# Quantised gate and up weights of a two-layer transformer kernel: integers made by TensorE transposes, or from a second load in the transposed layout

## The reference

```python
h_q = (rmsnorm(x) @ w_q.T); h_k = (ctx @ w_k.T); h_v = (ctx @ w_v.T)      # per head
x = x + hidden + softmax(h_q h_k^T + position_bias, masked) @ h_v @ w_out.T

def fake_quant(t, axis):
    s = jnp.max(jnp.abs(t), axis=axis, keepdims=True) / QMAX
    s = jnp.maximum(s, 1e-08)
    return jnp.clip(jnp.round(t / s), -QMAX - 1.0, QMAX) * s

gate = fake_quant(y, -1) @ fake_quant(w_gate, 1).T
up = fake_quant(y, -1) @ fake_quant(w_up, 1).T
x = x + fake_quant(silu(gate) * up, -1) @ fake_quant(w_down, 1).T
```

## Time and profile before

| what | us |
|---|---|
| median of 3 runs | 1104.09 |
| lowest and highest of them | 1101.44 and 1105.84 |
| the profiled execution | 1102.04 |
| its span, first to last instruction | 1100.3 |

### The profile page before, as it was taken

The page is one execution under the profiler, slowest core; times in us unless marked ns, Lnnn a source line. Parts: engine busy times, 40 slices in busy tenths (PEclk is TensorE's granted clock), DMA queues, the critical chain, the costliest instruction groups (busy, mean ns, idle before and its releaser), DMA issues. The chain is left out here.

```text
span 1100.3 us, 18306 instructions
## 1 busy us (share of the span) xinstructions
PE 999.7 (91%) x6010; PEld 844.0 (77%) x6010; DVE 706.1 (64%) x1844; ACT 515.7 (47%) x1330; POOL 469.3 (43%) x362
## 2 busy tenths in 40 slices
PE   4999999999999999999999999999999999565465
PEld 3888888888888888888888888888878887333353
DVE  6566565656576767586555665665676575587384
ACT  3454444444444554445543543553555344167251
POOL 5554444444444545434444354353444352344200
PEclk9999999999999999999999999999999999799577
DMA  6433333323333323334232132222212220000002
GB/s 205 146 94 94 95 95 93 94 93 95 93 96 96 92 89 97 117 99 133 59 105 82 32 104 70 72 82 82 72 62 82 82 63 23 20 1 1 1 1 77
DMA packets 50412, 87.71 MB, mean 80 GB/s; under 512 B 6368, under 2 KB 15200, under 8 KB 50336
## 3 DMA queue, kind: packets, MB, share of 16 engines
q1 hardware_dynamic: 50336, 86.76, 25.5%
HBM read 84.64 MB, written 2.10 MB: 79 GB/s over the span
## 5 line engine op out<-in xcount | busy, mean ns | idle before, releaser
L540 POOL TENSOR_TENSOR wq_lo<-raw_q,wq_hi 128x512 fp32r<-128x512 f32 x64 | 82.8, 1293 | 263.6 <-DVE prob L1213 257.3
L1493 PE MATMUL pX<-wv_lo,cT_hi 128*128 128x256 f32 x512 | 149.3, 292 | 0.2 <-ACT q_sb L678 0.2
L1196 DVE TENSOR_TENSOR score<-pS,b_mask 128x512 f32<-128x512 f32 x64 | 44.2, 691 | 161.4 <-PE pS L1671 148.1
L802 ACT ACTIVATE prob<-score,neg_max 128x128 f32<-128x128 f32 x256 | 99.7, 391 | 97.2 <-DVE neg_max L1199 97.2
L1494 PE MATMUL pX<-wv_hi,cT_lo 128*128 128x256 f32 x512 | 144.0, 281 | 0.0
L1495 PE MATMUL pX<-wv_hi,cT_hi 128*128 128x256 f32 x512 | 144.0, 281 | 0.0
L540 POOL TENSOR_TENSOR wv_lo<-raw_v,wv_hi 128x1024 fp32r<-128x1024 f32 x32 | 77.6, 2425 | 124.9 <-ACT wv_hi L678 124.9
L678 ACT ACTIVATE v_sb<-pX 128x512 f32<-128x512 f32 x64 | 38.2, 597 | 163.2 <-PE pX L1495 163.2
L1493 PE MATMUL pX<-xT_lo,wq_hi 128*128 128x512 f32 x256 | 106.0, 414 | 6.1 <-POOL wq_lo L540 5.1
L1493 PE MATMUL oacc<-wo_lo,aT_hi 128*128 128x512 f32 x256 | 100.5, 393 | 5.1 <-DVE aT_lo L1191 3.8
L1493 PE MATMUL pX<-cT_lo,wk_hi 128*128 128x512 f32 x256 | 105.0, 410 | 0.0
(11 more groups left out here) (276 smaller groups left out, 2387.1 us busy)
## 6 DMA issues: line engine op xcount, KB each, us to landing
raw_k<-in_wk SPq DMA_DIRECT2D x64, 256.0 KB, 2.9
raw_q<-in_wq SPq DMA_DIRECT2D x64, 256.0 KB, 3.5
raw_v<-in_wv SPq DMA_DIRECT2D x32, 512.0 KB, 4.2
raw_o<-in_wo SPq DMA_DIRECT2D x64, 256.0 KB, 2.7
b_raw<-in_bias SPq DMA_DIRECT2D x64, 64.0 KB, 2.8
g_raw<-in_w_gate SPq DMA_DIRECT2D x16, 172.0 KB
g_raw<-in_w_up SPq DMA_DIRECT2D x16, 172.0 KB
f_raw<-in_w_down SPq DMA_DIRECT2D x4, 688.0 KB, 4.7
```

The costliest lines, as they stand in the source:

```text
L540: g.tensor_tensor(w_lo[c][:], w_raw[c][:], w_hi[c][:].bitcast(F32), ALU.subtract).then_inc(s_w_lo[c], 1)
L802: e = a.activation(prob[:, b, :], score[:, b, :], ACT.Exp, bias=neg_max[:, b:b + 1], accum_out=row_sum[:, b:b + 1])
L1196: v.tensor_tensor(score[:], pS[:].rearrange("p (b s) -> p b s", b=HB), b_mask[:], ALU.add).then_inc(s_scored, 1)
L1493: mm(dst, lh, rl, start=start, stop=False, skip_group_check=lint)
```

## The change

The host passes the gate and up weights a second time, transposed: partition p holds, for each of four blocks of 128 input columns, the 86 weights of a slice (`rows_across`). Each of steps 0 to 31 loads such a slice too (`load_across`, 128 x 344 f32, 172 KB), behind the load of `raw_k`, once `s_g_mag` says that the slice before has been used. The load of `g_raw` now waits for the maximum alone (`s_g_max`). `g_mag`, `g_q` and their instructions go, as do the reciprocal at L1178 and TensorE's four transposes with their wait. VectorE instead runs `scaled_rows` at the end of its step: when ScalarE has copied the spread steps (`s_g_out`), it takes the reciprocal of 86 of them on all partitions, multiplies the transposed weights by it, and adds the rounding constant. ScalarE takes the constant off one step later and writes `w_rowT` straight from SBUF. VectorE's loop over groups of four steps covers steps 4 to 15 instead of 4 to 19; the rest is written out.

```diff
--- before.py
+++ after.py
@@ -70,8 +70,9 @@
         g_raw = sbuf("g_raw", [P, D])
-        g_mag = sbuf("g_mag", [P, D])
-        g_q = sbuf("g_q", [P, D], BF16)
+        gT_raw = sbuf("gT_raw", [P, KT, FR])
+        g_scaled = sbuf("g_scaled", [P, KT, FR])
+        g_inv = sbuf("g_inv", [P, 1, FR])
...
@@ -438,8 +440,14 @@
             def load_rows(i, src, t):
 
                 if later(i):
+                    sp.wait_ge(s_g_max, i)
+                sp.dma_start(g_raw[0:FR, :], src[t]).then_inc(s_g_in, 16)
+
+            def load_across(i, srcT, t):
+
+                if later(i):
                     sp.wait_ge(s_g_mag, i)
-                sp.dma_start(g_raw[0:FR, :], src[t]).then_inc(s_g_in, 16)
+                sp.dma_start(gT_raw[:], srcT[t]).then_inc(s_gT_in, 16)
...
             load_rows(0, w_gate, 0)
+            load_across(0, w_gateT, 0)
             context(1)
...
                 if unless_last(n + 2):
                     load("k", n + 2, head2)
+                if rows is not None and later(n):
+                    load_across(n, (w_gateT, w_upT)[rows], n - rows * (H // 2))
                 if odd and unless_last(n + 3):
...
@@ -816,12 +827,11 @@
-                if rows is not None:
-
-                    act.wait_ge(s_g_mag, n + 1)
-                    if later(n):
-                        act.wait_ge(s_g_trans, n)
-                    a.activation(g_q[0:FR, :], g_mag[0:FR, :], ACT.Copy, bias=-MAGIC).then_inc(s_g_q, 1)
+                if later(n) and (rows is not None or n == H):
+                    whose = (n - 1) // (H // 2) if isinstance(n, int) else rows
+                    act.wait_ge(s_g_mag, n)
+                    a.activation(w_rowT[whose][:, :, rows_of(n - 1 - whose * (H // 2))], g_scaled[:], ACT.Copy,
+                                 bias=-MAGIC).then_inc(s_g_int, 1)
...
                 if rows is not None:
                     cols = rows_of(n - rows * (H // 2))
-                    act.wait_ge(s_g_trans, n + 1)
-                    copy(w_row[rows][:, cols], pX1[:, 0:FR])
-                    copy(w_rowT[rows][:, :, cols],
-                         g_trans_bank[:, 0:KT * FR].rearrange("p (k r) -> p k r", k=KT)).then_inc(s_g_out, 1)
+                    act.wait_ge(s_g_row, n + 1)
+                    copy(w_row[rows][:, cols], pX1[:, 0:FR]).then_inc(s_g_out, 1)
...
@@ -1171,26 +1179,33 @@
                 dve.wait_ge(s_g_in, 16 * (n + 1))
-                v.tensor_reduce(f_s[0:FR, 0:1], g_raw[0:FR, :], AX.X, ALU.max, apply_absolute_value=True)
+                v.tensor_reduce(f_s[0:FR, 0:1], g_raw[0:FR, :], AX.X, ALU.max,
+                                apply_absolute_value=True).then_inc(s_g_max, 1)
                 dve.drain()
                 v.tensor_scalar(f_s[0:FR, 1:2], f_s[0:FR, 0:1], 1.0 / QMAX, 1e-8, ALU.mult, ALU.max)
                 dve.drain()
-                v.reciprocal(f_s[0:FR, 2:3], f_s[0:FR, 1:2])
                 if later(n):
-                    dve.wait_ge(s_g_trans, n)
+                    dve.wait_ge(s_g_row, n)
                 v.tensor_scalar(f_diag[0:FR, 0:FR], ident[0:FR, 0:FR], f_s[0:FR, 1:2], None,
                                 ALU.mult).then_inc(s_g_diag, 1)
-                dve.drain()
+
+            def scaled_rows(n, whose):
+
+                dve.wait_ge(s_g_out, n + 1)
+                v.reciprocal(g_inv[:, 0, :], w_row[whose][:, rows_of(n - whose * (H // 2))])
+                dve.drain()
+                dve.wait_ge(s_gT_in, 16 * (n + 1))
                 if later(n):
-                    dve.wait_ge(s_g_q, n)
-                v.tensor_scalar(g_mag[0:FR, :], g_raw[0:FR, :], f_s[0:FR, 2:3], MAGIC,
-                                ALU.mult, ALU.add).then_inc(s_g_mag, 1)
+                    dve.wait_ge(s_g_int, n)
+                v.tensor_tensor(g_scaled[:], gT_raw[:], g_inv[:].to_broadcast([P, KT, FR]), ALU.mult)
+                dve.drain()
+                v.tensor_scalar(g_scaled[:], g_scaled[:], MAGIC, None, ALU.add).then_inc(s_g_mag, 1)
...
@@ -1241,21 +1256,23 @@
                         v.tensor_scalar(top_flat[:, tile], pick[:, r, ::-1], LOWEST, None, ALU.not_equal)
+                if rows is not None:
+                    scaled_rows(n, rows)
                 early_end(n)
                 second_x_end(n)
                 if isinstance(n, int) and n in (1, H - 1):
                     add_norm(n // (H - 1))
...
-            quad(0)
-            with dve.Fori(1, SECOND_X // 4 - 1) as q:
-                quad(q)
-            for q in range(SECOND_X // 4 - 1, H // 4):
-                quad(q)
+            quad(0, 0)
+            with dve.Fori(1, H // 8) as q:
+                quad(q, 0)
+            for q in range(H // 8, H // 4):
+                quad(q, 1)
...
@@ -1718,12 +1735,8 @@
                     pe.wait_ge(s_k, n + 2)
-                    mm(pX1[:, 0:FR], ones[0:FR, :], f_diag[0:FR, 0:FR], start=True, stop=True)
-                    pe.wait_ge(s_g_q, n + 1)
-                    for kt in range(KT):
-                        last = tr(g_trans_bank[:, kt * FR:(kt + 1) * FR], g_q[0:FR, kt * P:(kt + 1) * P],
-                                  ident_b[0:FR, 0:FR])
-                    last.then_inc(s_g_trans, 1)
+                    mm(pX1[:, 0:FR], ones[0:FR, :], f_diag[0:FR, 0:FR], start=True,
+                       stop=True).then_inc(s_g_row, 1)
...
+    def rows_across(w):
+
+        return w.reshape(H // 2, FR, KT, P).transpose(0, 3, 2, 1)
```

More of the change, by code:

```diff
@@ L50, in layers_kernel @@
 def layers_kernel(nc, x, cT, mask, bias, ln_w, wq, wk, wv, wo, w_gate, w_up, w_down,
-                  conv_w, gamma, beta, router_w, router_b, lora_a, lora_b, out):
+                  w_gateT, w_upT, conv_w, gamma, beta, router_w, router_b, lora_a, lora_b, out):
     ctx = ExitStack()
@@ L284, in layers_kernel @@
         s_g_in = sem("g_in")
+        s_gT_in = sem("gT_in")
         s_g_mag = sem("g_mag")
+        s_g_max = sem("g_max")
+        s_g_row = sem("g_row")
         s_g_out = sem("g_out")
         s_g_proj = sem("g_proj")
-        s_g_q = sem("g_q")
-        s_g_trans = sem("g_trans")
+        s_g_int = sem("g_int")
         s_gate = sem("gate")
@@ L396, in layers_kernel @@
         h_blocks = range(6), range(6, IT)
-        g_trans_bank = pX1[:].bitcast(BF16)[:, NH:2 * NH]
         def later(n):
@@ L1191, in attended_low, with step @@
                 v.tensor_tensor(aT_lo[:], pT[:], aT_hi[:].bitcast(F32), ALU.subtract).then_inc(s_a_lo, 1)
-            def step(n, half, q, j, rows=False):
+            def step(n, half, q, j, rows=None):
                 dve.wait_ge(s_b_mask, n + 1)
@@ L1201, in step @@
                     attended_low(n - 1)
-                if rows:
+                if rows is not None:
                     rows_of_gate(n)
@@ L1247, in step, with quad @@
                     add_norm(n // (H - 1))
-            def quad(q):
+            def quad(q, rows):
                 for j in range(4):
-                    step(4 * q + j, 0, q, j, rows=True)
+                    step(4 * q + j, 0, q, j, rows)
             dve.wait_ge(s_cT_lo, KT)
-            quad(0)
-            with dve.Fori(1, SECOND_X // 4 - 1) as q:
-                quad(q)
-            for q in range(SECOND_X // 4 - 1, H // 4):
-                quad(q)
+            quad(0, 0)
[3 more added lines that the diff above has]
+                quad(q, 1)
             dve.wait_ge(s_cT_lo, 2 * KT)
@@ L1922 @@
         "w_down": host("L0_ffn_w_down"),
+        "w_gateT": rows_across(host("L0_ffn_w_gate")),
+        "w_upT": rows_across(host("L0_ffn_w_up")),
         "conv_w": rows(host("L1_xattn_conv_w")),
```

## The result

| | before | after |
|---|---|---|
| median of the runs made together (4 each), us | 1102.97 | 1117.2 |
| lowest and highest of them | 1101.44 and 1105.84 | 1116.52 and 1118.47 |
| the profiled execution, and its span | 1102.04, 1100.3 | 1117.56, 1115.7 |

After against before is 1.0134, with a 95% interval of 1.0111 to 1.0157: slower by about 14 us. That is the sign that was forecast, and 4 us more than 1113.

A forecast was written before the change was run, and what follows sets the result against it. TensorE's list of matmuls was taken to set the time (busy 91%). Terms -6.7 + 4.5 + 11.9 = +9.7 us gave 1111.7 on the profiled execution, 1113.8 on the median, stated as 1113; range 1102 to 1122.

The forecast's parts named there:

- The transposes, -6.7 us: TensorE, seams of steps 0 to 31: removing four transposes gains 0.21 us a step, 6.7 us in all.
- The reciprocal, 0.74 us between 0.25 and 0.91: VectorE's new reciprocal of 86 elements: taken at 0.74 us, 0.25 at the least, 0.91 at the most.
- rival 1: Reciprocal slower, 0.8 to 0.9 us: steps 0.31 us late, total +15.1 us, 1119 to 1123; chance 0.22.
- rival 2: Hardly any change: reciprocal 0.25 us, `add_norm` keeps its turn, 6.6 us lost against 6.7 gained, 1104; chance 0.22.
- Rival 3: Faster: cover before TensorE needs `aT_lo` is wider, hiding nearly all new work, 1097.5 us; chance 0.08.
- Ordinary steps, 0.14 us late: VectorE at each step's end: 1.80 us of new work against 1.66 available, 4.5 us over 32 steps.
- Steps 20 to 22, 2.4 + 0.6 us: VectorE's statistics of steps 20 and 21 (2.4 us) and aggregation of step 22 (0.6) now stand behind `scaled_rows` and are lost.
- Step 1 and step 31, 3.8 and 3.1 us: `add_norm` behind `scaled_rows`: 1.9 us if VectorE keeps its turn, 5.6 and 4.3 if GpSimd gets in; midpoints taken.
- Step 0, 2.0 us: New multiply and add fall beside GpSimd's `wk_lo` and `cT_lo`: between 0 and 2.6 us lost, 2.0 taken.
- The loads, nothing: SyncE's 32 added loads of 172 KB arrive well before use and were costed at nothing.
- From step 32 on nothing changes: Steps from 32 on were expected to keep their times, no cost or gain.

The follow-up runs named there:

- experiment 1: Kernel before, with TensorE's four transposes left out in each of steps 0 to 31: 1099.31 us, ratio to before 0.9965.
- experiment 6: Changed kernel with VectorE's loop over steps 4 to 15 written out: 1115.88 us, ratio to before 1.0117.
- experiment 9: Changed kernel with `scaled_rows` moved into the next step except for steps 23 to 27 and 31, VectorE's loop kept: 1103.33 us, ratio to before 1.0004.
- experiment 11: Changed kernel with TensorE repeating query matmuls in its long pauses of steps 2 and 32: 1117.63 us, ratio to before 1.0125.
- experiment 7: Kernel before, with the 32 loads of transposed weights added and their data unused: 1101.78 us, ratio to before 0.9988.
- experiment 3: Changed kernel with GpSimd's `wv_lo` of steps 1 and 31 held until `add_norm` ends: 1114.06 us, ratio to before 1.0093.
- experiment 4: Changed kernel with the reciprocal of the 86 spread steps done twice: 1193.19 us, ratio to before 1.0816.
- experiment 5: Changed kernel with all of `scaled_rows` done one step later, behind `rows_of_gate`: 1104.44 us, ratio to before 1.0007.
- experiment 10: Changed kernel with `scaled_rows` in the next step except for steps 23 to 27, VectorE's loop written out: 1099.52 us, ratio to before 0.9969.
- experiment 2: Changed kernel with `add_norm` and the batch-norm work of steps 20 to 22 ahead of `scaled_rows`: 1104.66 us, ratio to before 1.0018.
- experiment 8: Changed kernel with `scaled_rows` in the next step except for steps 23 to 27 and 31, VectorE's loop written out: 1100.89 us, ratio to before 0.9981.

## Why the prediction was right, and where its terms were off

The forecast of a slowdown stands, its place (`aT_lo` late for the outputs) and its reason too. The size is less good: the sum said +9.7 us, the medians +14.2. By its own steps:

- **The transposes, -6.7 us:** -5.05 by experiment 1. The pitch of 0.15 was the right reading; the seam's 0.22 was not all theirs. It came from one step, 42, whose seam is 1.02 us; those at the ends of steps 33 to 36, without rows too, are 1.25.
- **The reciprocal, 0.74 us between 0.25 and 0.91:** 0.692. The slope of two short rows, pulled towards the floor, was close; from 4 elements to 86 it is 6.4 ns each. Rivals 1 and 2 both fall by this number. That rival 1's sum, +15.1, is nearer to the +14.2 than mine is luck: it had a longer reciprocal in every step, and the time went elsewhere. Rival 3 falls too: VectorE's lateness shows in the outputs as soon as it grows by 0.1 us, in the steps of the loop. The rule of the Trainium skill, "VectorE: DVE Perf Modes", which stands there in "First, the fixed hardware budget", read as eight cycles an element, gave an estimated 0.85 us; the trace doesn't agree with that reading. Multiply and addition came to 0.52 (0.52 taken) and 0.34 (0.40).
- **Ordinary steps, 0.14 us late:** the new work was put at 1.80 us against 1.66 of cover. From the copy's end to the bias addition it measures 288.29 - 286.58 = 1.71, and the outputs are on time in written-out steps and 0.1 late in the loop. In time: steps 3 to 20 and 24 to 31, 26 in all, came out at +0.31 where the sum had 26 x (0.14 - 0.21) = -1.8. What it lacked is VectorE's loop, to which it gave no price, since before it is hidden: experiment 6 puts it at 1.8 us of these 2.1.
- **Steps 20 to 22, 2.4 + 0.6 us:** +1.12, +1.13 and +0.69 in steps 21 to 23, 2.9 us together against 3.0 - 3 x 0.07 = 2.8 in the sum: right.
- **Step 1 and step 31, 3.8 and 3.1 us:** +6.95 and, with step 33, +4.16. These are the terms that failed. I left open whether GpSimd gets in between `add_norm`'s instructions and took midpoints; it does, both times, and the upper ends, 5.6 and 4.3, were close for the lateness (5.02 and 4.06 us at the outputs' start). A midpoint between two mechanisms is neither of them. And step 2 had 2.0 us more, which no end held: TensorE's lower clock behind the pause. In step 32 the outputs were 1.6 us slower too, but most of that was not lost (experiments 9 and 11).
- **Step 0, 2.0 us:** +1.56, in the way described. The multiply takes 1.24 us and the addition 1.28 there, beside `wk_lo` and `cT_lo`:

```profile
44.01 1.29 POOL L551 TENSOR_TENSOR wk_lo<-raw_k,wk_hi 128x512 fp32r<-128x512 f32 x1
45.26 1.57 POOL L579 TENSOR_TENSOR cT_lo<-cT_raw,cT_hi 128x512 fp32r<-128x512 f32 x1
```

```profile
44.44 1.24 DVE L1200 TENSOR_TENSOR g_scaled<-gT_raw,g_inv 128x344 f32<-128x344 f32 x1
45.75 1.28 DVE L1202 TENSOR_SCALAR g_scaled<-g_scaled 128x344 f32<-128x344 f32 x1
```

- **The loads, nothing:** nothing (experiment 7).
- **From step 32 on nothing changes:** nearly. Step 49 is 1.15 us longer in after, and 1.1 to 1.2 in experiments 1, 3, 4, 5 and 10; it is as in before in 2, 6, 7, 8, 9 and 11. TensorE pauses there for 1.95 us (1.96 in before) ahead of the queries, and what differs is the granted clock behind it: 0.54 in one window of after, 1.00 in before.

```profile
742.70:744.70 2.00, 2.00 (x6) 0.54 0.67 152
```

```profile
726.70:728.70 2.00, 1.87 (x8) 1.00 0.54 172
```

It appears in kernels with nothing else in common, experiment 1 without any of the new work among them, so I take it for a matter of the execution and not of the change. There is one trace of each kernel; whether it changes between two executions of one kernel is not shown and stays open. Step 55 is 0.64 us longer in after and as much in experiments 2, 3 and 11, at a granted clock of 1.00; why is open too.

By steps the sum reads: forecast +9.7; step 2 adds 3.2 to it, 32 and 33 1.1, the ordinary steps 2.1, 34 to 62 1.7 (1.2 of it step 49), 21 to 23 0.1, and step 1 takes 0.4 off: 17.5, against 17.6 measured between the first and the last scores. The medians differ by 14.2, since the stretch behind step 63 happened to be shorter. So the size was missed by one question, what GpSimd does while `add_norm` runs, and by one mechanism that was not in the list, what a pause does to TensorE's clock.

## What to carry to other kernels

Work that hangs on a late signal pins everything behind it in its engine's order: put what needs nothing new ahead of it, and place it by step, where that step has room. Two moved lines were worth 12.5 us here, and a placement by step, with VectorE's loop written out, turned a loss of 14 us into a gain of 3.6. Where two mechanisms price a step differently, decide between them from the instructions of both engines at that time, don't take the middle; and when an engine that sets the time is left waiting, count what it does afterwards too.

## What the runs showed that I had not expected

- **A pause of TensorE can cost more than its length.** Behind pauses of 1.84 us (experiment 3), 2.62 (experiment 4), 3.91 and 4.85 (after) the granted clock was 0.50 to 0.62 in windows of the outputs, and these took 4.20 to 4.86 us instead of 2.87 (up to 5.3 in experiments 4 and 6), so 1.3 to 2.4 us more. With the pause filled by matmuls whose results are overwritten, the clock stayed at 1.00. Over steps 0 to 62 of all 13 traces the granted clock fell 28 times, each time at or behind a pause of 1.78 to 5.41 us. None of the 62 pauses of 1.0 to 1.75 us had a fall behind it, all seven from 3.8 us up had one, and those of 1.78 to 2.85 us went either way: 21 with a fall, 10 without.
- **Back-to-back instructions of VectorE don't hold GpSimd off.** `add_norm`'s four took 1.92 us alone and 4.93 and 3.98 with GpSimd waiting. For a single instruction it counts who starts first: an addition that started 0.03 us ahead of GpSimd's `wv_lo` took 0.34 us, those that started 0.2 us or more behind it 2.0 to 2.4.
- **0.7 us more in a chain cost 76 us in all** (experiment 4), because the addition of every second step started behind GpSimd's and TensorE's clock mostly fell behind the pause: a cliff 0.4 to 0.5 us from where the changed kernel stands.
- **VectorE's loop is free only under cover**: 0.1 us a step and 0.4 a turn once the steps have no slack.
